# A two-layer network over spikes: the first layer on w1 rows gathered per batch, places by one-hot products

## The chip, the core and the metric

One Trainium2 chip, and of it one core. The program is launched once and the metric is its device time in microseconds (us). The core has five engines that run side by side: TensorE (PE) for matrix products, VectorE (DVE), ScalarE (ACT), GpSimd (POOL) and SyncE (SP), which here only issues DMAs. DMAs are issued from the queues of SP, ACT and POOL and run on 16 DMA engines.

## The reference

```python
def cond(inputs, initial_state):                 # inputs = x, (2, 2048, 512); initial_state (2, 512)
    rates = relu(inputs) * 0.001
    c = initial_state[:, None, :] + cumsum(rates, axis=1)
    fl = floor(c)
    prev = concatenate([floor(initial_state)[:, None, :], fl[:, :-1, :]], axis=1)
    return (fl - prev) / 0.001                    # a spike where a channel's sum crosses a whole number

def ffn(x, w1, b1, w2, b2):                       # w1 (512, 2048), w2 (2048, 512), all float32
    h = relu(einsum('bsd,dw->bsw', x, w1) + b1)
    return einsum('bsw,wd->bsd', h, w2) + b2

out = x + ffn(cond(x, cond_1024), w1, b1, w2, b2)
```

Each of the 1,024 channels (2 batches of 512) starts in [0, 1) and crosses a whole number at most about once in its 2,048 tokens. So most tokens have no spike and get one same row (the *idle row*, relu(b1) w2 + b2); a token with one spike gets the idle row plus a row of a table with one row per channel; only tokens where several channels cross together (*general* tokens, up to 128 *slots* in all) need the two layers.

## The kernel before

x lies in SBUF as `x_sb[b]`, 128 partitions of 16 tokens; a *block* is the 16 tokens of a partition. The steps:

- SP loads x and the pairs of w1 transposed and w2 (`w_pairs`), then b2, then w1 itself in four parts (L306).
- PE forms the table of 512 rows in PSUM (`ps_table`, `table_part`, L833): 16 chunks of 4 products of 128x128x512, two passes each. Between the parts it runs small products that find the crossings: block sums, the block of each channel, the token within it, counts per token (`count_tokens`), numbers of the general tokens (`count_before`), and the number given back to each channel (`give_back`).
- DVE finds for each channel the block (`find_blocks`), POOL gathers that block's 16 rates (L352), DVE finds the token (`find_tokens`) and the slot (`find_slots`; 0 for a channel that is alone). `first_spikes` and `second_spikes` (L634, L638) turn the slots of batch 0 and 1 into the one-hot matrix `spk_t`.
- After `second_spikes` DVE raises `adding` and adds the idle row to batch 0 and to half of batch 1 (`add_idle`, L697, from PSUM, 4 tokens a call); POOL, which waited for `adding`, does it for the other half of batch 1 (L364, a token a call). SP stores each quarter of a batch (L310, 1 MB, eight in all) in the written order (0,0) (0,1) (0,2) (0,3) (1,3) (1,0) (1,2) (1,1). A store waits for its quarter, and those behind it in SP's queue wait too.
- PE, after the table and w1: `first_layer` (L922, 16 chunks of four products of 128x128x128), in it `sum_rows` (rows of the slots), then `sum_checks`, then `second_layer` (L929, 16 products of 128x128x512). ACT applies relu between them (L466) and copies the four parts of the table out (L472).
- DVE between its calls of `add_idle`: `list_singles` (L646 to L653, where the table rows go), `find_members` (L658 to L661), `find_odd` and `count_crowd` (L665 to L672), `list_general` (L678 to L685, the rows of the slots), `judge`.
- POOL at the end, in this order: when batch 0 is stored, four scatter-adds of table rows into `out` (L357); the gather of the slots' rows of x (L376, `general_x`); when batch 1 is stored, four more scatter-adds; when the two layers are done, the scatter of the general rows (L387). SP waits for all of them.
- If a count shows that the shortcut does not hold, a slow path redoes every token (`redo`). It isn't taken with these inputs.

Each engine works its own list in order. `chain` makes an engine wait for the instruction just issued.

Of the kernel before, what the change touches and what calls it, by code (L numbers as in the profile page):

```python
# [18 lines left out]
def spike_ffn(nc, x, x_turned, cond, cond_cols, w1, w_pairs, b1_cols, b2, out):  # L19
# [35 lines left out]
    with ExitStack() as ctx:  # L55
# [27 lines left out]
        member = [sb(f"member{b}", [P, DC, P], BF16) for b in range(B)]  # L83
        facts = sb("facts", [P, NE, 3], BF16)
# [34 lines left out]
        batch_row = sb("batch_row", [P, NE])  # L119
        rates = sb("rates", [P, NE, BLK])  # L120
        climb = sb("climb", [P, NE, BLK])
        tokens_under = sb("tokens_under", [P, NE])
# [3 lines left out]
        slot = sb("slot", [P, NE])  # L126
# [9 lines left out]
        checks = sb("checks", [P, 2])  # L136
        slot_count = sb("slot_count", [P, 1])
        slot_place = sb("slot_place", [P, 2])
        slot_row = sb("slot_row", [P, 1])
        crowd = sb("crowd", [P, 1])  # L140
# [35 lines left out]
        ps_rows = ps_met[:, 4 * BLK + NE * 2 * BLK:4 * BLK + NE * 2 * BLK + 3]  # L176
# [7 lines left out]
        w1_in = [sem(f"w1_in{i}") for i in range(WQ)]  # L184
# [33 lines left out]
        members_ready = sem("members_ready")  # L218
# [12 lines left out]
        adding = sem("adding")  # L231
        idle_added = [[sem(f"idle_added{b}_{q}") for q in range(XQ)] for b in range(B)]
        idle_stored = [sem(f"idle_stored{b}") for b in range(B)]
        spk_ready = sem("spk_ready")
# [37 lines left out]
        def _(sp):  # L272
# [47 lines left out]
        def _(pool):  # L320
# [27 lines left out]
            for b in range(B):  # L348
                pool.wait_ge(sixteen_listed, b + 1)
                for c in range(DC):  # L350
# [3 lines left out]
                                            ).then_inc(sixteen_got[b], 16)  # L354

# [11 lines left out]

            pool.wait_ge(idle_copied, 1)
            pool.wait_ge(adding, 1)
# [21 lines left out]
            with pool.If(redo > 1):  # L391
                pool.wait_ge(singles_scattered, 16 * NE)
                pool.wait_ge(general_scattered, 16)
                pool.dma_start(own_init, cond.rearrange("(o b) d -> o b d", o=1).to_broadcast([P, B, D])).then_inc(
# [20 lines left out]
        def _(act):  # L415
# [614 lines left out]
```

## Time and profile before

| | us |
|---|---|
| median of 3 runs (lowest, highest) | 107.22 (106.98, 108.17) |
| the profiled execution | 108.13 |
| its span, first to last instruction | 106.4 |
| busy in the span: PE / DVE / POOL / ACT | 94.6 / 67.9 / 36.6 / 36.2 |

The profile is one execution. The span is what the engines' records cover; 1.73 us of the profiled execution lie outside it. Times of rows count from the start of the span. The busy time of an engine is a sum over stages, and a stage's end is read from what its last wait was for.

### The profile page before, as it was taken

Reading aid. Unit: us, or ns where it says so; the run is one execution under the profiler, and the core shown is the slowest. Engines: PE = TensorE matmul, PEld = TensorE weight load, DVE = VectorE, ACT = ScalarE, POOL = GpSimd, SP = SyncE. Lnnn points to the kernel's source line nnn. Section 1 sums busy time; section 2 is a strip of 40 time slices with the busy share of each in tenths; the row PEclk is TensorE's granted clock in tenths of the full one; section 3 lists DMA queues with packets and bytes.
Section 4 is the critical chain, followed back from the end, with each engine's and each line's share of the span. In section 5 each row is a group of like instructions: output and inputs, shape, how many; then the busy total and the mean of one; then the engine's idle time right before and its main releaser. Section 6 shows DMA issues by size and latency. Waiting matters only on the chain.

```text
span 106.4 us, 1159 instructions
## 1 busy us (share of the span) xinstructions
PE 94.6 (89%) x375; PEld 52.2 (49%) x375; DVE 67.9 (64%) x137; ACT 36.2 (34%) x66; POOL 36.6 (34%) x41
## 2 busy tenths in 40 slices
PE   5999999999999999999895999999999999995000
PEld 5844444444644444634251444599999644441000
DVE  2348999888599999385445599999998700022000
ACT  2867515514382353189740000059443200000000
POOL 6200000000077500038300199960018780088720
PEclk9999999999999999999999999999999999999965
DMA  2999999999999999999992000499999999947850
GB/s 90 276 351 407 421 419 411 405 410 411 407 408 408 395 391 413 398 390 386 374 367 91 0 0 6 197 441 397 434 404 397 391 202 354 242 93 99 103 108 9
DMA packets 10028, 31.66 MB, mean 298 GB/s; under 512 B 1671, under 2 KB 1799, under 8 KB 8994
## 3 DMA queue, kind: packets, MB, share of 16 engines
q1 hardware_dynamic: 8304, 29.63, 72.4%
q0 software_dynamic: 1568, 1.90, 10.9%
q8 instruction: 5, 0.08, 0.3%
q10 hardware_dynamic: 146, 0.01, 0.1%
q14 instruction: 5, 0.04, 0.1%
HBM read 21.58 MB, written 10.75 MB: 304 GB/s over the span
## 4 chain that ended last, share of the span: by engine, by line
PE 43%; DVE 15%; POOL 13%; issue 12%; DMA 10%; POOLq 2%; DVEq 0%
PE ps_table L833 37%; DVE x_sb L697 8%; POOL out L357 8%; DMA rates<-in_x_turned,sixteen_at 5%; DMA out<-x_sb 5%; DVE spk_t L638 4%; PE ps_small L934 4%; POOL rates L352 3%; PE ps_turn L870 2%; POOLq L55 2%; POOL out L387 1%; POOL general_x L376 1%; DVE under L579 1%; DVE blocks_under L582 1%; POOLq L267 0%
## 5 line engine op out<-in xcount | busy, mean ns | idle before, releaser
L833 PE MATMUL ps_table<-w_sb 128*128 128x512 f32 x128 | 57.5, 602 | 0.1
L833 PEld LDWEIGHTS ps_table<-w_sb 128*128 128x128 f32 x128 | 24.0, 193 | 27.0 <-issue 26.2
L352 POOL DMA_INDIRECT rates<-in_x_turned,sixteen_at x8 | 9.6, 1198 | 36.9 <-DVE sixteen_at L583 35.0
L428 ACT ACTIVATE w_sb<-w_sb,b_col 128x512 f32<-128x512 f32 (+2 forms) x19 | 12.2, 642 | 16.7 <-DMA w_sb<-in_w_pairs 16.7
L357 POOL DMA_INDIRECT out<-w_sb,to_single x8 | 12.5, 1561 | 15.7 <-DMA out<-x_sb 13.8
L569 DVE SCALAR_TENSOR_TENSOR total_two<-x_sb,total_two 128x1024 f32<-128x1024 f32 x14 | 17.1, 1224 | 1.1 <-DMA x_sb<-in_x 0.6
L929 PE MATMUL ps_table<-w_sb 128*128 128x512 f32 x32 | 14.0, 595 | 0.0
L697 DVE TENSOR_TENSOR x_sb<-x_sb,ps_idle 128x2048 f32<-128x2048 f32 x6 | 13.4, 2277 | 0.1
L364 POOL TENSOR_TENSOR x_sb<-x_sb,idle_row 128x512 f32<-128x512 f32 x8 | 10.1, 1289 | 9.1 <-DVEq L738 9.1
L429 ACT ACTIVATE w_sb<-w_sb,minus_relu_b 128x512 f32<-128x512 f32 (+2 forms) x19 | 12.3, 649 | 0.6
L929 PEld LDWEIGHTS ps_table<-w_sb 128*128 128x128 f32 x32 | 6.0, 190 | 7.2 <-issue 6.9
L466 ACT ACTIVATE w_sb<-ps_turn,b_col 128x128 f32<-128x128 f32 x8 | 2.9, 367 | 17.9 <-PE ps_turn L922 17.8
L922 PE MATMUL ps_turn<-spk_t,w_sb 128*128 128x128 f32 x64 | 8.5, 276 | 0.0
L922 PE MATMUL ps_small<-spk_t,w_sb 128*128 128x128 f32 x64 | 8.5, 275 | 0.0
L528 DVE SCALAR_TENSOR_TENSOR idle_part<-w_sb,relu_b,idle_part 128x512 f32<-128x512 f32 x9 | 6.8, 760 | 2.1 <-DMA w_sb<-in_w_pairs 2.0
L922 PEld LDWEIGHTS ps_turn<-spk_t,w_sb 128*128 128x128 f32 x64 | 7.9, 192 | 0.5 <-issue 0.5
L922 PEld LDWEIGHTS ps_small<-spk_t,w_sb 128*128 128x128 f32 x64 | 7.8, 192 | 0.0
L753 DVE TENSOR_TENSOR general_x<-general_x,b_row 128x512 f32<-128x512 f32 x1 | 0.7, 693 | 9.9 <-DMA general_x<-in_x,from_general 9.9
L934 PE MATMUL ps_small<-ones 128*128 128x128 f32 x16 | 3.8, 431 | 1.1 <-POOLq L329 1.1
L638 DVE SCALAR_TENSOR_TENSOR spk_t<-name_f,slot,spk_t 128x128 f32<-128x128 f32 x4 | 4.2, 1104 | 0.0
L466 ACT ACTIVATE w_sb<-ps_small,b_col 128x128 f32<-128x128 f32 x8 | 2.9, 367 | 3.2 <-PE ps_small L922 3.2
L934 PEld LDWEIGHTS ps_small<-ones 128*128 128x128 f32 x16 | 3.5, 330 | 1.1 <-POOLq L329 1.1
(124 smaller groups left out, 54.2 us busy)
## 6 DMA issues: line engine op xcount, KB each, us to landing
x_sb<-in_x SPq DMA_DIRECT2D x16, 512.0 KB, 14.3
out<-x_sb SPq DMA_DIRECT2D x8, 1024.0 KB, 4.8
w_sb<-in_w_pairs SPq DMA_DIRECT2D x15, 512.0 KB, 15.5
w_sb<-in_w SPq DMA_DIRECT2D x4, 1024.0 KB, 16.0
w_sb<-in_w_pairs SPq DMA_DIRECT2D x2, 256.0 KB, 3.1
b_row<-in_b SPq DMA_DIRECT2D x1, 256.0 KB, 15.6
rates<-in_x_turned,sixteen_at POOLq DMA_INDIRECT x8, 5.9
out<-w_sb,to_single POOLq DMA_INDIRECT x8, 6.6
```

The lines of the kernel that those rows point to most:

```text
L352: pool.indirect_dma_start(out=rates[:, col, :], out_offset=None, in_=x_sixteen, in_offset=bass.IndirectOffsetOnAxis(ap=sixteen_at[:, col:c ...
L357: pool.indirect_dma_start(out=out_rows, out_offset=bass.IndirectOffsetOnAxis(ap=to, axis=0), in_=row, in_offset=None, bounds_check=last_ro ...
L364: last = pool.tensor_tensor(x_sb[b][:, t, :], x_sb[b][:, t, :], idle_row[:, :], ALU.add)
L428: chain(act.activation(weights, weights, ACT.Relu, bias=b1_col[:, m:m + 1], scale=PER_DT))
L429: act.activation(weights, weights, ACT.Identity, bias=minus_relu_b1[:, m:m + 1]).then_inc(table_hidden_ready, 1)
L569: chain(dve.scalar_tensor_tensor(out=total_two[b][:, :, :], in0=tokens, scalar=0.0, in1=total_two[b][:, :, :], op0=ALU.max, op1=ALU.add))
L638: last = dve.scalar_tensor_tensor(out=spk_t[:, c, :], in0=slot_name, scalar=slot[:, DC + c:DC + c + 1], in1=spk_t[:, c, :], op0=ALU.is_equ ...
L697: last = dve.tensor_tensor(tokens, tokens, along(ps_idle[:, :], end - begin), ALU.add)
L833: last = pe.matmul(ps_table[c][:, :], table_hidden[:, m, c * P:(c + 1) * P], w2_sb[:, m, :], start=(m == 0), stop=(m == FC - 1))
L922: last = pe.matmul(ps_hidden[m % 2][:, 0:P], w1_sb[:, c, m * P:(m + 1) * P], spk_t[:, c, :], start=(c == 0), stop=(c == DC - 1))
L929: last = pe.matmul(ps_out[:, :], hidden[m], w2_sb[:, m, :], start=(m == 0), stop=(m == FC - 1))
L934: pe.matmul(ps_small[:, 0:P], ones[:, :], ones[:, :], start=True, stop=True)
```

## The change

w1 is no longer loaded whole (it is, from POOL, only on the slow path). For each batch, the channels that have a slot (*members*) get a *place* from 1 to 128: DVE counts them per partition (`count_members`), PE sums the counts over the partitions before, DVE makes a one-hot matrix of the places (`place_members`), PE multiplies it with the channel's facts (channel number, slot, row; `sum_places`), and DVE reads off for each place the row of w1, the token's row and a one-hot matrix of the slot (`list_places`). POOL gathers the 128 rows of w1 of each batch (8 KB each, 1 MB) by `get_w1`. The first layer is then two products a chunk, one for each batch (`general_first`), and runs two chunks ahead of the second (`general_second`), one after the other on PE.

Other things move. `spk_t` is not made outside the slow path. DVE starts `add_idle` after `list_places(1)`; `list_general` stands after the first call of `add_idle` and waits for `sum_rows`, which PE does between chunks 14 and 15 of the table; `list_singles` stands before the fourth call, `find_odd` and `count_crowd` after it. `adding` is gone: POOL issues `get_w1(0)`, `get_w1(1)` and the gather of `general_x` (which waits for `list_general`), and then adds its half of batch 1. ACT copies the first part of the table before the first relu, and `sum_checks` stands after chunk 5 of the second layer.

```diff
-            for i in range(WQ):
-                part = slice(i * (F // WQ), (i + 1) * (F // WQ))
-                sp.dma_start(w1_sb[:, :, part], w1.rearrange("(c p) f -> p c f", p=P)[:, :, part]).then_inc(w1_in[i], 16)
...
+            def get_w1(b):
+                pool.wait_ge(places_listed, b + 1)
+                pool.indirect_dma_start(out=w1_got_rows[b], out_offset=None, in_=w1,
+                                        in_offset=bass.IndirectOffsetOnAxis(ap=w1_at[b][:, :], axis=0)
+                                        ).then_inc(w1_got[b], 16)
...
+            get_sixteens(0)
+            get_sixteens(1)
+            get_w1(0)
             pool.wait_ge(idle_copied, 1)
-            pool.wait_ge(adding, 1)
+            get_w1(1)
+            pool.wait_ge(general_listed, 1)
+            pool.indirect_dma_start(out=general_x[:, :], out_offset=None, in_=x_rows,
+                                    in_offset=bass.IndirectOffsetOnAxis(ap=from_general[:, :], axis=0)
+                                    ).then_inc(general_got, 16)
             add_idle(1, 12, 16)
             add_idle(1, 8, 12)
             pool.wait_ge(singles_listed, 1)
             for b in range(B):
-                if b == 1:
-                    pool.wait_ge(general_listed, 1)
-                    pool.indirect_dma_start(out=general_x[:, :], out_offset=None, in_=x_rows,
-                                            in_offset=bass.IndirectOffsetOnAxis(ap=from_general[:, :], axis=0)
-                                            ).then_inc(general_got, 16)
                 pool.wait_ge(idle_stored[b], 16 * XQ)
...
+            act.wait_ge(table_summed, FC)
+            act.activation(table_row[0], ps_table[0][:, :], ACT.Copy).then_inc(table_rows_ready, 1)
             for m in range(FC):
-                if 1 <= m <= DC:
-                    act.activation(table_row[m - 1], ps_table[m - 1][:, :], ACT.Copy).then_inc(table_rows_ready, 1)
+                if 1 <= m < DC:
+                    act.activation(table_row[m], ps_table[m][:, :], ACT.Copy).then_inc(table_rows_ready, 1)
...
+                with nc.allow_low_precision(reason="whole numbers that the type holds"):
+                    chain(dve.tensor_reduce(facts_high[:, mine, 1:2].rearrange("p e o -> p (e o)"), slot_part[:, :, :],
+                                            AXIS.X, ALU.add))
+
+            def count_members(b):
+
+                mine = own(b)
+                chain(dve.tensor_scalar(is_member[:, mine], facts_high[:, mine, 1:2].rearrange("p e o -> p (e o)"), 0.5, None,
+                                        ALU.is_gt))
+                chain(dve.tensor_tensor_scan(member_run[b][:, :], ones[:, 0:DC], is_member[:, mine], 0.0, ALU.mult, ALU.add))
+                dve.sem_inc(members_counted, 1)
+                with nc.allow_low_precision(reason="whole numbers that the type holds"):
+                    chain(dve.tensor_reduce(facts_low[:, mine, 2:3].rearrange("p e o -> p (e o)"),
+                                            token_under[:, mine, 1:BLK], AXIS.X, ALU.add))
+
+            def place_members(b):
+                mine = own(b)
+                dve.wait_ge(members_before, b + 1)
+                chain(dve.scalar_tensor_tensor(out=place[:, mine], in0=member_run[b][:, :], scalar=ps_members[b],
+                                               in1=is_member[:, mine], op0=ALU.add, op1=ALU.mult))
+                chain(dve.tensor_tensor(place_hot[b][:, :, :], over(place[:, mine], P), along(slot_name, DC), ALU.is_equal))
+                dve.sem_inc(places_ready, 1)
+
+            def list_places(b):
+                dve.wait_ge(places_summed, b + 1)
+                dve.tensor_copy(w1_at[b][:, :], ps_places[b][:, 0:1]).then_inc(places_listed, 1)
+                dve.tensor_copy(place_fact[b][:, 1:2], ps_places[b][:, 2:3])
+                dve.tensor_scalar(place_slot[b][:, :], slot_name, ps_places[b][:, 1:2], None, ALU.is_equal).then_inc(
+                    slots_placed, 1)
...
-                chain(dve.tensor_reduce(tokens_under[:, :], token_under[:, :, 1:BLK], AXIS.X, ALU.add))
-                chain(dve.scalar_tensor_tensor(out=row_at[:, :], in0=blocks_under[:, :], scalar=float(BLK),
-                                               in1=tokens_under[:, :], op0=ALU.mult, op1=ALU.add))
+                chain(dve.tensor_tensor(row_at[:, :], facts_high[:, :, 2:3].rearrange("p e o -> p (e o)"),
+                                        facts_low[:, :, 2:3].rearrange("p e o -> p (e o)"), ALU.add))
                 chain(dve.tensor_scalar(not_single[:, :], met[:, :], 1.0, FAR, ALU.not_equal, ALU.mult))
-                chain(dve.tensor_tensor(row_at[:, :], row_at[:, :], batch_row[:, :], ALU.add))
                 dve.tensor_tensor(to_single[:, :], row_at[:, :], not_single[:, :], ALU.add).then_inc(singles_listed, 1)
-            def find_members():
-
-                for b in range(B):
-                    chain(dve.tensor_tensor(member[b][:, :, :], over(slot[:, own(b)], P), along(slot_name, DC), ALU.is_equal))
-                    chain(dve.tensor_scalar(facts[:, own(b), 1:2].rearrange("p e o -> p (e o)"), blocks_under[:, own(b)],
-                                            float(b * P), None, ALU.add))
-                chain(dve.tensor_copy(facts[:, :, 2:3].rearrange("p e o -> p (e o)"), tokens_under[:, :]))
-                dve.sem_inc(members_ready, 1)
...
+                chain(dve.tensor_scalar(under_zero[:, :], start_c[:, :], 0.0, float(2 * P), ALU.is_lt, ALU.mult))
+                chain(dve.scalar_tensor_tensor(out=over_two[:, :], in0=over_two[:, :], scalar=float(2 * P), in1=under_zero[:, :],
+                                               op0=ALU.mult, op1=ALU.add))
+                chain(dve.tensor_reduce(checks[:, 3:4], over_two[:, :], AXIS.X, ALU.add))
...
                 chain(dve.tensor_tensor(checks[:, 0:1], many_run[0][:, BLK - 1:BLK], many_run[1][:, BLK - 1:BLK], ALU.add))
+                for b in range(B):
+                    chain(dve.tensor_copy(checks[:, b + 1:b + 2], member_run[b][:, DC - 1:DC]))
                 dve.sem_inc(odd_ready, 1)
...
             find_slots(0)
-            first_spikes()
+            count_members(0)
+            place_members(0)
             find_tokens(1)
+            list_places(0)
             find_general(1)
             number_general(1)
             find_slots(1)
-            second_spikes()
-            dve.sem_inc(adding, 1)
+            count_members(1)
+            place_members(1)
+            list_places(1)
             add_idle(0, 0, 4)
+            list_general()
             add_idle(0, 4, 8)
             add_idle(0, 8, 12)
+            list_singles()
             add_idle(0, 12, 16)
-            list_singles()
-            find_members()
-            add_idle(1, 0, 4)
             find_odd()
             count_crowd()
-            list_general()
+            add_idle(1, 0, 4)
             add_idle(1, 4, 8)
             judge()
             dve.wait_ge(general_got, 16)
...
+            def count_members(b):
+                pe.wait_ge(members_counted, b + 1)
+                pe.wait_ge(sums_ready, B)
+                pe.matmul(ps_members[b], upper_b[:, :], member_run[b][:, DC - 1:DC], start=True, stop=True).then_inc(
+                    members_before, 1)
+            def sum_places(b):
+                pe.wait_ge(places_ready, b + 1)
+                for facts in (facts_high, facts_low):
+                    for c in range(DC):
+                        last = pe.matmul(ps_places[b], place_hot[b][:, c, :], facts[:, b * DC + c, :],
+                                         start=(facts is facts_high and c == 0), stop=(facts is facts_low and c == DC - 1))
+                last.then_inc(places_summed, 1)
+                pe.wait_ge(slots_placed, B)
+                for b in range(B):
+                    last = pe.matmul(ps_rows, place_slot[b][:, :], place_fact[b][:, :], start=(b == 0), stop=(b == B - 1))
                 last.then_inc(rows_summed, 1)
...
+            def general_first(m):
+                if m >= 2:
+                    pe.wait_ge(hidden_ready, m - 1)
+                for b in range(B):
+                    last = pe.matmul(ps_hidden[m % 2][:, 0:P], w1_got_rows[b][:, m * P:(m + 1) * P], place_slot[b][:, :],
+                                     start=(b == 0), stop=(b == B - 1))
+                last.then_inc(hidden_summed, 1)
+            def general_second(m):
+                if m == 0:
+                    pe.wait_ge(table_rows_ready, 1)
+                pe.wait_ge(hidden_ready, m + 1)
+                last = pe.matmul(ps_out[:, :], hidden[m], w2_sb[:, m, :], start=(m == 0), stop=(m == FC - 1))
+                if m == FC - 1:
+                    last.then_inc(out_summed, 1)
...
             give_back(0)
             turn_blocks(1)
-            table_part(12, 1, DC)
+            table_part(12, 1, 2)
+            count_members(0)
+            table_part(12, 2, 3)
+            sum_places(0)
+            table_part(12, 3, DC)
             count_tokens(1)
             table_part(13, 0, 1)
             count_before(1)
             table_part(13, 1, 2)
             give_back(1)
-            table_part(13, 2, DC)
+            table_part(13, 2, 3)
+            count_members(1)
+            table_part(13, 3, DC)
+            sum_places(1)
             table_chunk(14)
+            sum_rows()
             table_chunk(15)
+            pe.wait_ge(general_listed, 1)
+            for b in range(B):
+                pe.wait_ge(w1_got[b], 16)
+            general_first(0)
+            general_first(1)
+            for m in range(FC):
+                general_second(m)
+                if m + 2 < FC:
+                    general_first(m + 2)
+                if m == 5:
+                    sum_checks()
```

## Rows read from the trace of the kernel before

**Rows 1.** The page of the profile: the span.

```profile
span 106.4 us, 1159 instructions
```

**Rows 2.** Chain that ended last, in order of time: start us, us, what.

```profile
50.79 5.51 DMA rates<-in_x_turned,sixteen_at
...
73.64 4.97 DMA out<-x_sb
...
87.92 5.06 issue
...
100.67 1.03 POOL out L387
```

**Rows 3.** POOL in order of time: start us, us, instruction [idle before it <-releaser].

```profile
79.44 1.61 POOL L357 DMA_INDIRECT out<-w_sb,to_single  x1 [8.54 <-DMA out<-x_sb]
...
93.20 1.56 POOL L357 DMA_INDIRECT out<-w_sb,to_single  x1 [5.28 <-DMA out<-x_sb]
```

**Rows 4.** First and last store of `out` on SP, and their us to landing.

```profile
L310 SPq DMA_DIRECT2D out<-x_sb x1: 361/361/361, 67.0 to 67.0; - x1
...
DMA to landing us min/median/max: 4.0/4.0/4.0
...
L310 SPq DMA_DIRECT2D out<-x_sb x1: 332/332/332, 84.0 to 84.0; - x1
...
DMA to landing us min/median/max: 8.9/8.9/8.9
```

**Rows 5.** Stretches: us, busy of PE, PEld, DVE, ACT, POOL, PEclk, DMA share, GB/s.

```profile
57.00:67.00 10.00, 9.21 (x31) 4.19 (x32) 8.19 (x15) 0.00 (x0) 6.16 (x5) 1.00 0.01 4
...
69.00:93.00 24.00, 24.00 (x159) 18.73 (x159) 14.62 (x33) 7.82 (x20) 9.15 (x7) 1.00 1.02 361
...
71.00:79.00 8.00, 8.00 (x75) 8.00 (x74) 7.51 (x15) 5.21 (x13) 0.00 (x0) 1.00 1.02 424
```

**Rows 6.** DVE in order of time, columns as in rows 3.

```profile
13.67 0.75 DVE L528 SCALAR_TENSOR_TENSOR idle_part<-w_sb,relu_b,idle_part 128x512 f32<-128x512 f32 x1
...
64.75 8.87 DVE L697 TENSOR_TENSOR x_sb<-x_sb,ps_idle 128x2048 f32<-128x2048 f32 x4
...
73.54 0.28 DVE L646 TENSOR_TENSOR count_part<-ps_met,token_hot 128x128 f32<-128x128 f32 x1
...
75.09 0.17 DVE L653 TENSOR_TENSOR to_single<-row_at,not_single 128x8 int32<-128x8 f32 x1
...
75.18 0.68 DVE L658 TENSOR_TENSOR member<-slot,name_f 128x512 bf16<-128x512 f32 x1
...
79.57 0.16 DVE L665 TENSOR_TENSOR over_two<-block_sum,theta_sum 128x8 f32<-128x8 f32 x1
...
80.25 0.16 DVE L672 TENSOR_TENSOR checks<-many_run 128x1 f32<-128x1 bf16 x1
...
80.55 0.16 DVE L678 TENSOR_SCALAR slot_count<-ps_met 128x1 f32<-128x1 f32 x1
...
81.66 0.15 DVE L685 TENSOR_TENSOR to_general<-slot_row,none_far 128x1 int32<-128x1 f32 x1
```

**Rows 7.** Lines L638, L364, L697: ns min/median/max, first and last start us.

```profile
L638 DVE SCALAR_TENSOR_TENSOR spk_t<-name_f,slot,spk_t x4: 352/1352/1359, 60.6 to 63.5; 128x128 f32<-128x128 f32 x4
...
L364 POOL TENSOR_TENSOR x_sb<-x_sb,idle_row x8: 1265/1280/1318, 60.8 to 69.6; 128x512 f32<-128x512 f32 x8
...
L697 DVE TENSOR_TENSOR x_sb<-x_sb,ps_idle x6: 2273/2274/2287, 64.7 to 81.7; 128x2048 f32<-128x2048 f32 x6
```

**Rows 8.** PE in order of time, columns as in rows 3; two passes a float32 product.

```profile
59.94 8.83 PE L833 MATMUL ps_table<-w_sb 128*128 128x512 f32 x20
...
68.61 1.05 PE L922 MATMUL ps_turn<-spk_t,w_sb 128*128 128x128 f32 x8
...
79.33 0.34 PE L909 MATMUL ps_met<-facts,member 128*128 128x3 bf16 x8
...
83.33 13.98 PE L929 MATMUL ps_table<-w_sb 128*128 128x512 f32 x32
```

More of the change, by code:

```diff
@@ L82, in spike_ffn @@
         grid = [sb(f"grid{b}", [P, 2 * BLK], BF16) for b in range(B)]
-        member = [sb(f"member{b}", [P, DC, P], BF16) for b in range(B)]
-        facts = sb("facts", [P, NE, 3], BF16)
+        member_run = [sb(f"member_run{b}", [P, DC], BF16) for b in range(B)]
+        place_hot = [sb(f"place_hot{b}", [P, DC, P], BF16) for b in range(B)]
+        facts_high = sb("facts_high", [P, NE, 3], BF16)
+        facts_low = sb("facts_low", [P, NE, 3], BF16)
+        w1_at = [sb(f"w1_at{b}", [P, 1], I32) for b in range(B)]
+        place_fact = [sb(f"place_fact{b}", [P, 2]) for b in range(B)]
+        place_slot = [sb(f"place_slot{b}", [P, P]) for b in range(B)]
         spk_t = sb("spk_t", [P, DC, P])
@@ L175, in spike_ffn @@
         ps_back = ps_met[:, 4 * BLK:4 * BLK + NE * 2 * BLK].rearrange("p (e k) -> p e k", e=NE)
-        ps_rows = ps_met[:, 4 * BLK + NE * 2 * BLK:4 * BLK + NE * 2 * BLK + 3]
+        ps_rows = ps_turn[:, (B + 1) * BLK:(B + 1) * BLK + 2]
+        ps_members = [ps_turn[:, b:b + 1] for b in range(B)]
+        ps_places = [ps_turn[:, (b + 1) * BLK:(b + 1) * BLK + 3] for b in range(B)]
+        w1_got_rows = [w1_sb[:, b, :] for b in range(B)]
         ps_hidden = [ps_turn, ps_small]
@@ L183, in spike_ffn @@
         w2_first_in = sem("w2_first_in")
-        w1_in = [sem(f"w1_in{i}") for i in range(WQ)]
+        w1_in = sem("w1_in")
+        w1_got = [sem(f"w1_got{b}") for b in range(B)]
         start_in = sem("start_in")
@@ L596, in pick_blocks @@
                                   ALU.is_equal).then_inc(blocks_picked, 1)
+                chain(dve.tensor_scalar(facts_high[:, own(b), 2:3].rearrange("p e o -> p (e o)"), blocks_under[:, own(b)],
+                                        float(BLK), float(b * S), ALU.mult, ALU.add))
             def find_tokens(b):
@@ L630, in find_slots @@
                 chain(dve.tensor_tensor(slot_part[:, :, :], ps_back[:, mine, 0:BLK], token_hot[:, mine, :], ALU.mult))
-                chain(dve.tensor_reduce(slot[:, mine], slot_part[:, :, :], AXIS.X, ALU.add))
-            def first_spikes():
-                chain(dve.tensor_tensor(spk_t[:, :, :], over(slot[:, own(0)], P), along(slot_name, DC), ALU.is_equal))
-            def second_spikes():
-                for c in range(DC):
-                    last = dve.scalar_tensor_tensor(out=spk_t[:, c, :], in0=slot_name, scalar=slot[:, DC + c:DC + c + 1],
-                                                    in1=spk_t[:, c, :], op0=ALU.is_equal, op1=ALU.add)
-                    if c < DC - 1:
-                        last.then_inc(dve_step, 1)
-                steps[0] += DC - 1
-                last.then_inc(spk_ready, 1)
+                with nc.allow_low_precision(reason="whole numbers that the type holds"):
+                    chain(dve.tensor_reduce(facts_high[:, mine, 1:2].rearrange("p e o -> p (e o)"), slot_part[:, :, :],
+                                            AXIS.X, ALU.add))
@@ L963, in _ @@
             give_back(1)
-            table_part(13, 2, DC)
+            table_part(13, 2, 3)
+            count_members(1)
+            table_part(13, 3, DC)
+            sum_places(1)
             table_chunk(14)
+            sum_rows()
             table_chunk(15)
-            pe.wait_ge(spk_ready, 1)
-            for i in range(WQ):
-                pe.wait_ge(w1_in[i], 16)
-            for m, last in enumerate(first_layer(hidden_ready, 0)):
-                last.then_inc(hidden_summed, 1)
-                if m == 11:
-                    sum_rows()
-            sum_checks()
-            second_layer(hidden_ready, 0).then_inc(out_summed, 1)
+            pe.wait_ge(general_listed, 1)
[9 more added lines that the diff above has]
+                    sum_checks()
             pe.wait_ge(redo_ready, 1)
```

47 lines of the change are left out of this document (22 added, 25 removed).

## The prediction

> **What bounds the kernel now.** I read the span first [rows 1]: 106.4 us of the 108.13 of its execution, and then the chain of waits from its end. By busy time PE looks like the bound, but the end does not hang on PE. The last link is POOL's scatter of the general rows, issued at 100.67 [rows 2]; it stands behind four scatter-adds, which POOL begins at 93.20, when batch 1's stores have landed [rows 3]. The last store is issued at 84.03 and takes 8.9 us, so it lands at 92.9 [rows 4]. From that landing to the end of the span are 106.4 - 92.9 = 13.5 us, all POOL issue and the last landing. PE's second layer ends at 83.33 + 13.98 = 97.3 [rows 8], over 3 us before POOL could use it.
>
> Why does the last store take 8.9 us and the first 4.0 [rows 4]? The stretches tell: from 57 to 67 the DMA engines carry nothing (4 GB/s), from 69 to 93 they are full (share 1.02) [rows 5]. So the stores are a stream that a full DMA works off. Between 71 and 79, with stores alone, it moves 424 GB/s [rows 5]: 1.05 MB are 2.47 us a store, eight are 19.8. The first store's 4.0 us leave 1.5 beside its 2.47; I put 0.8 ahead of the data and 0.7 behind. Then data flow from 67.85 to 92.2, 24.4 us: 19.8 of stores and 4.6 of the batch 0 scatter-adds that go between them (POOL starts them at 79.44, when the store issued at 73.64 has landed [rows 2, 3]). Thus the end is: start of the stream, plus 24.4 if it never runs dry, plus 14.2. The question for each edit is whether the stream starts sooner, and whether it runs dry.
>
> **The change, part by part.**
>
> *w1's load goes, gathers come.* The 4.2 MB ended before 57 [rows 5], ten us ahead of the stores: nothing waited for them, gain 0. The rates' gather may land sooner than its 5.51 us [rows 2], but DVE is then busy with `place_members(0)` until about 56.1, against 56.4 before: 0 to 0.3, I take 0.2, spent in the next step.
>
> *From slots to stores.* Before, DVE had batch 1's slots at 60.6 and then four calls of L638 held it until 64.75 [rows 6, 7]. Now come two small DVE operations (0.2 each), a PE product (0.2), two DVE operations (0.25, and 0.68 for a 128x512 comparison [rows 6]), PE's eight small products (0.34 [rows 8]), `list_places` (0.45), with five hand-overs of 0.1: 2.6, to about 63.1. The first store is issued 2.25 later, at 65.35 instead of 67.05: 1.7 sooner.
>
> *PE meanwhile.* Table passes last 8.83 / 20 = 0.44 [rows 8]. Chunk 14 ended about 68.6 - 8 x 0.44 = 65.1; PE now waits some 0.3 at three or four of the added products, 0.9 together: 66.0. `sum_rows` 0.4: 66.4.
>
> *`list_general` moved up* stands behind the first `add_idle`, which ends at 65.35, and waits to 66.5, and then takes 80.55 to 81.8 = 1.26 [rows 6] less one operation, 1.05. Behind it waits the second `add_idle`: 67.55 to 69.8, and the third to 72.05 (2.2 a call [rows 6]). The stream, fed at 65.35, has its first store out by 68.6, or by 70.0 with the second w1 gather in its way (2.47 more), and gets the second from 70.65. Before, it had by then worked 2.8 us at stores, now 2.47: the lead of 1.7 is gone. The gather of `general_x` now also falls into the stream; by size a quarter of a store, 0.65.
>
> *POOL's half of batch 1 moves from 60.8 to 69.* It waits for `general_listed` (67.5), issues the gather (1.03 like L387 [rows 2]) and adds until 69 + 8 x 1.28 = 79.2. SP takes (1,3) and (1,2) only behind others, so that alone costs 0. What it meets costs: before, POOL added beside L638 and L697 only. The row of L638 shows what happens: the first call, ahead of POOL's, took 352 ns; the next three 1352 each, one POOL call (1280) apiece [rows 7], though the same operation on four times the columns takes 0.75 [rows 6]. L697 beside the same POOL calls was not slowed (2273 to 2287 in all six [rows 7]). L638 reads two tensors from SBUF, L697 one from SBUF and one from PSUM. So I expect that a DVE operation with two SBUF tensors waits for POOL's current call. In `list_singles` these are two (`row_at`, `to_single`), in `find_odd` and `count_crowd` three, two of them TENSOR_TENSOR and one of L638's own kind. Before, all of them ran with POOL silent, 0.17 each [rows 6].
>
> The Trainium skill, SBUF — State Buffer, section Who interferes with whom, says that a VectorE instruction with two SBUF inputs contends with a GpSimd one that reads SBUF, and the loser waits for the whole instruction; rows 7 agree for SCALAR_TENSOR_TENSOR. It extends this to `tensor_tensor` and, in a two-port mode, to `tensor_scalar`, which no row here shows; by it the sum below holds, and without it that of the first rival.
>
> Each wait lies between 0.2 and 1.28; the first of a group I take at half a call, 0.65, one behind another at 0.9. `list_singles` free: 73.54 to 75.26 is 1.72 [rows 6] for seven operations, five are left: 1.2, so 73.2; with the waits 74.8 (bounds 73.6 and 75.8). The fourth `add_idle` ends at 77.0 instead of 75.4. `find_odd` and `count_crowd`, 0.85 before [rows 6] and two copies more, 1.25, plus about 2 of waits until POOL ends at 79.5: 80.2. The last two calls end at 82.5 and 84.7 (before 79.6 and 84.0).
>
> *The stream again.* (0,1), (0,2) and `general_x` from 70.65: 76.2. (0,3), issued at 77.1, from 77.9: dry for 1.6. With (1,3) to 82.8. (1,0) from 83.2: dry 0.4. Then three stores, 7.4, and the scatter-adds' 4.6 (POOL begins them at 82.2, when (0,3) has landed): 95.2, landing 95.9. Before 92.9: +3.0, less the 0.2 of the rates: **+2.8**. The span would be 109.2. As the profiled execution lies 0.9 over the median of the runs shown, I set the change against the median: 107.22 + 2.8 = 110.0. With the waits' bounds +1.8 to +3.8.
>
> *The two layers.* A chunk is now four passes of 128 columns, 4 x 0.112 (L922's twelve chunks of eight passes lie between 68.61 and 79.33 [rows 8]), and two of 512 columns, 0.88: 1.32, times 16 is 21.2. It begins when the table ends, at 69.9, or the second w1 gather lands: 62.7 plus between 4.0 (a whole 1 MB store [rows 4]) and 5.5 + 2.5 (a small gather [rows 2] plus a store's data): 66.7 to 70.7; I take 70. `sum_checks` waits for `odd_ready` (80.2), PE stands about 1.5. End 93, against 97.3. That is 4 us gained where 3 were idle: worth 0. POOL issues the general scatter 100.67 - 92.9 = 7.8 us behind the last store's landing, so at 103.7: ten us of cover. If that were gone, each us of PE past it would be added.
>
> **Rivals.** *DVE does not wait for POOL* (L638's wait is its own kind's). Speaks for it that TENSOR_TENSOR with two SBUF tensors has no row beside POOL's adds. `add_idle` ends at 75.4, 78.95 and 81.2, the stream is dry only to 70.65, and its last data flow at 76.2 + 5 x 2.47 + 4.6 = 93.1, landing 93.8: +0.9, 108.1 (from +0.3 to +1.4, with one of L638's kind waiting).
>
> *The last store's landing follows its issue, not the backlog.* If the 8.9 us came from the scatter-adds' nearness alone, and DVE keeps clear of POOL, the last store is issued at 81.2 instead of 84.0 and the end comes 2.8 sooner: 104.4; faster from the point where the last `add_idle` ends before 82.9. Against it: the DMA share of 1.02 from 69 to 93.
>
> *The gather of w1 rows is far slower* (128 rows of 8 KB, some perhaps the same row), or DVE's waits are whole POOL calls each: past 111. The first decides only if the second gather lands after 80, ten us beyond the bounds.
>
> That the slow path is taken and w1 is loaded after all would show as hundreds of us; by the reference a channel rises 0.4 x 0.001 a token, so 512 cross 0.2 times a token and some 0.18 of about 420 crossings a batch meet another, near 76 members against 128 places: I leave it out.
>
> **Chances.** The forecast, DVE held by POOL and a stream run dry, 0.55 (109.0 to 111.0); DVE free 0.22 (107.5 to 108.6); landing follows issue 0.17 (104.4 to 106.1); worse 0.06. About 1% is what a measurement here can tell from no change, 106.15 to 108.3: slower gets the forecast, the worse cases and a third of the second, 0.68; same two thirds of the second, 0.15; faster the third, 0.17. The range holds the first two and the edges of the others: 106.6 to 111.3.
>
> **What the profile would show.** First store issued near 65.4, second near 69.8. POOL's adds from 69 to 79, and beside them DVE operations of 8 columns that last near 1 us instead of 0.17. DMA stretches that are not full near 69 to 70 and 77 to 78. Last store issued near 84.7, landing near 96, 13.5 before the end. PE's layers end near 93 with a wait for `odd_ready`. I am wrong if those small operations stay at 0.17, if the last store lands before 92, or if PE's end is the last wait.

## The result and the profile after

The changed kernel takes 111.34 us (median of 4 runs, 110.85 to 112.07), the kernel before 107.55 (4 runs): ratio 1.0356, 95% interval 1.0269 to 1.0444. It is slower, as forecast, but by 3.8 us and not by 2.8, and a little past the upper end of the range (111.3). The profiled execution took 110.85, its span is 109.1.

The end of the chain of waits (start us, us, what), which answers to [rows 2]:

```profile
66.82 4.39 DVE x_sb L724 x2
...
71.77 6.19 DVE row_at L686
...
78.37 6.92 issue
...
92.50 4.53 issue
...
104.66 1.03 POOL out L401
```

One VectorE operation, `row_at` in `list_singles`, stands in the chain with 6.19 us. Then "issue" 6.92: POOL waits until batch 0 is stored, and its last quarter, (0,3), is issued only at 80.6, behind the fourth `add_idle`, and takes 3.9 us to land. The tail is as before: POOL waits for the last store (the 4.53), scatters four times, and scatters the general rows.

VectorE in order of time (start us, us, instruction, in brackets idle time before it and what ended it), which answers to [rows 6]:

```profile
62.22 2.28 DVE L724 TENSOR_TENSOR x_sb<-x_sb,ps_idle 128x2048 f32<-128x2048 f32 x1
...
65.76 0.16 DVE L708 TENSOR_SCALAR slot_count<-ps_turn 128x1 f32<-128x1 f32 x1 [1.26 <-PE ps_turn L952]
...
66.73 4.48 DVE L724 TENSOR_TENSOR x_sb<-x_sb,ps_idle 128x2048 f32<-128x2048 f32 x2
71.13 0.29 DVE L684 TENSOR_TENSOR count_part<-ps_met,token_hot 128x128 f32<-128x128 f32 x1
...
71.77 6.18 DVE L686 TENSOR_TENSOR row_at<-facts_high,facts_low 128x8 f32<-128x8 bf16 x1
...
77.98 0.17 DVE L688 TENSOR_SCALAR not_single<-met 128x8 f32<-128x8 f32 x1
...
78.27 2.28 DVE L724 TENSOR_TENSOR x_sb<-x_sb,ps_idle 128x2048 f32<-128x2048 f32 x1
...
80.47 0.16 DVE L692 TENSOR_TENSOR over_two<-block_sum,theta_sum 128x8 f32<-128x8 f32 x1
```

`row_at` adds 8 columns of two SBUF tensors; the operations of this size in the kernel before took 0.17 [rows 6]. `count_part`, just ahead of it, has 128 columns, but one of its two inputs lies in PSUM, and it takes 0.29, as before (0.28). POOL in the same stretch, which answers to [rows 3] and to the row of L364 in [rows 7]:

```profile
68.06 9.85 POOL L376 TENSOR_TENSOR x_sb<-x_sb,idle_row 128x512 f32<-128x512 f32 x8
...
85.28 1.60 POOL L369 DMA_INDIRECT out<-w_sb,to_single  x1 [7.37 <-issue]
...
97.26 1.54 POOL L369 DMA_INDIRECT out<-w_sb,to_single  x1 [4.76 <-DMA out<-x_sb]
```

The eight adds run from 68.06 to 77.91, one about every 1.23 us, and `row_at`, which came at 71.77, as the third ended and the fourth began, ends at 77.95. It was held over all five that were left. The fourth `add_idle` of batch 0 stood behind it (78.27 instead of about 72.3), and with it the rest of the output. Stretches (us, busy of PE, PEld, DVE, ACT, POOL, granted clock, DMA share, GB/s), to set beside [rows 5]:

```profile
69.00:77.00 8.00, 7.66 (x36) 4.87 (x36) 7.93 (x5) 4.26 (x10) 8.00 (x8) 1.00 0.96 402
...
77.00:81.00 4.00, 1.80 (x11) 1.13 (x9) 3.86 (x8) 0.73 (x2) 0.92 (x1) 1.00 0.00 0
...
81.00:93.00 12.00, 11.21 (x45) 7.24 (x46) 6.07 (x10) 2.20 (x6) 6.30 (x4) 0.86 0.99 388
...
83.00:85.00 2.00, 2.00 (x7) 1.31 (x6) 2.00 (x2) 0.37 (x1) 0.00 (x0) 0.55 1.06 438
```

From 77 to 81 the DMA engines carry nothing, in the middle of the stream that was full from 69 to 93 before. The first store, (0,3) and the last one (SP; ns, start us, and us to landing), the first and last of which answer to [rows 4]:

```profile
L316 SPq DMA_DIRECT2D out<-x_sb x1: 348/348/348, 64.5 to 64.5; - x1
...
DMA to landing us min/median/max: 7.4/7.4/7.4
...
L316 SPq DMA_DIRECT2D out<-x_sb x1: 332/332/332, 80.6 to 80.6; - x1
...
DMA to landing us min/median/max: 3.9/3.9/3.9
...
L316 SPq DMA_DIRECT2D out<-x_sb x1: 623/623/623, 86.3 to 86.3; - x1
...
DMA to landing us min/median/max: 10.7/10.7/10.7
```

The last store lands at 86.3 + 10.7 = 97.0 and not at 92.9; the span ends 12.1 later.

### The profile page after: what moved, and what is told of

Its sections match the earlier page's. It is cut to its first block, busy times and chain, and to the rows that moved or that the text cites. A ratio compares the mean times of both kernels' runs of the same rounds, so it can differ in the third digit from the quotient of the medians.

```text
span 109.1 us, 1075 instructions
## 1 busy us (share of the span) xinstructions
PE 90.7 (83%) x325; PEld 46.1 (42%) x325; DVE 70.9 (65%) x148; ACT 36.5 (33%) x66; POOL 38.9 (36%) x43
## 4 chain that ended last, share of the span: by engine, by line
PE 46%; DVE 17%; issue 15%; POOL 10%; ACT 6%; POOLq 2%; DVEq 0%
PE ps_table L862 39%; POOL out L369 8%; DVE row_at L686 6%; DVE x_sb L724 4%; PE ps_small L993 3%; ACT w_sb L444 3%; ACT w_sb L443 2%; PE ps_turn L899 2%; POOLq L55 2%; DVE place_hot L673 1%; PE ps_idle L888 1%; POOL out L401 1%; DVE under L599 1%; ACT block_sum L453 1%; POOLq L277 1%
## 5 line engine op out<-in xcount | busy, mean ns | idle before, releaser
L862 PE MATMUL ps_table<-w_sb 128*128 128x512 f32 x128 | 58.0, 600 | 0.0
L862 PEld LDWEIGHTS ps_table<-w_sb 128*128 128x128 f32 x128 | 23.2, 190 | 24.2 <-issue 23.2
L443 ACT ACTIVATE w_sb<-w_sb,b_col 128x512 f32<-128x512 f32 (+2 forms) x19 | 12.2, 643 | 17.6 <-DMA w_sb<-in_w_pairs 17.5
L967 PE MATMUL ps_table<-w_sb 128*128 128x512 f32 x32 | 17.5, 634 | 0.1
L724 DVE TENSOR_TENSOR x_sb<-x_sb,ps_idle 128x2048 f32<-128x2048 f32 x6 | 13.5, 2282 | 0.1
L959 PEld LDWEIGHTS ps_small<-place_slot,w_sb 128*128 128x128 f32 x32 | 5.2, 209 | 3.9 <-issue 3.4
L959 PEld LDWEIGHTS ps_turn<-place_slot,w_sb 128*128 128x128 f32 x32 | 4.9, 197 | 4.4 <-issue 3.9
L784 DVE TENSOR_TENSOR w_sb<-ps_table,general_x 128x512 f32<-128x512 f32 x1 | 0.7, 692 | 8.8 <-PE ps_table L967 8.8
L686 DVE TENSOR_TENSOR row_at<-facts_high,facts_low 128x8 f32<-128x8 bf16 x1 | 6.2, 6178 | 0.0
L364 POOL DMA_INDIRECT w_sb<-in_w,w_at x2 | 1.9, 942 | 11.0 <-DVE w_at L678 11.0
L485 ACT ACTIVATE w_sb<-ps_table 128x512 f32<-128x512 f32 x1 | 0.6, 600 | 15.4 <-PE ps_table L862 15.4
L967 PEld LDWEIGHTS ps_table<-w_sb 128*128 128x128 f32 x32 | 5.4, 209 | 0.7 <-ACT w_sb L481 0.4
L959 PE MATMUL ps_turn<-place_slot,w_sb 128*128 128x128 f32 x32 | 5.2, 287 | 0.2 <-DMA w_sb<-in_w,w_at 0.2
L959 PE MATMUL ps_small<-place_slot,w_sb 128*128 128x128 f32 x32 | 5.3, 293 | 0.0
```

The lines of the kernel that those rows point to most:

```text
L443: chain(act.activation(weights, weights, ACT.Relu, bias=b1_col[:, m:m + 1], scale=PER_DT))
L686: chain(dve.tensor_tensor(row_at[:, :], facts_high[:, :, 2:3].rearrange("p e o -> p (e o)"), facts_low[:, :, 2:3].rearrange("p e o -> p (e ...
L724: last = dve.tensor_tensor(tokens, tokens, along(ps_idle[:, :], end - begin), ALU.add)
L862: last = pe.matmul(ps_table[c][:, :], table_hidden[:, m, c * P:(c + 1) * P], w2_sb[:, m, :], start=(m == 0), stop=(m == FC - 1))
L959: last = pe.matmul(ps_hidden[m % 2][:, 0:P], w1_got_rows[b][:, m * P:(m + 1) * P], place_slot[b][:, :], start=(b == 0), stop=(b == B - 1))
L967: last = pe.matmul(ps_out[:, :], hidden[m], w2_sb[:, m, :], start=(m == 0), stop=(m == FC - 1))
```

## The experiments

Two theories. **A**: the loss is the hold of one operation behind POOL's adds, which empties the stream of stores. **B**: the loss is what the change put into the stream and ahead of it, the two gathers of w1 rows, the early gather of `general_x` and the wait of `list_general`.

**e1_singles_first: `list_singles` into VectorE's idle time.**

```diff
             add_idle(0, 0, 4)
+            list_singles()
             list_general()
             add_idle(0, 4, 8)
             add_idle(0, 8, 12)
-            list_singles()
             add_idle(0, 12, 16)
```

> One call moved: the five operations of list_singles stand before list_general, where DVE stood idle for 1.26 us waiting for the rows of the slots, and POOL does not add there. Theory A (one VectorE operation, row_at, stood behind all of POOL's remaining adds for 6.18 us and emptied the stream of stores): row_at takes about 0.17; find_odd's first operation now meets POOL's adds at about 73.4 and stands until they end near 78, so that part of the loss stays: last store issued near 83.5 instead of 86.3, time 106.5 to 108.5 against 111.3 of the changed kernel. Rival B (the loss comes from what the change put in the DMA stream, two gathers of w1 rows and the early general_x gather, about 5.6 us of DMA work, and from the wait for list_general): none of that moves, 110.5 to 112.

107.53 us, ratio to the kernel before 1.0019 (0.9971 to 1.0067). One call of five small operations, moved, takes back the whole loss. The VectorE row that now meets POOL's adds:

```profile
74.19 4.64 DVE L692 TENSOR_TENSOR over_two<-block_sum,theta_sum 128x8 f32<-128x8 f32 x1
```

`over_two` has two float32 inputs from SBUF and is held as `row_at` was, 4.64 us, to the end of the adds. B is out as the main cause: all that it names is still there. The hold, too, is still there for another operation, but it comes only when the fourth `add_idle` is through, and (0,3) is issued at 74.3.

**e2_none_beside_pool: nothing with two SBUF tensors beside POOL's adds.**

```diff
             number_general(0)
+            find_odd()
             find_slots(0)
...
             place_members(1)
+            count_crowd()
             list_places(1)
             add_idle(0, 0, 4)
+            list_singles()
             list_general()
             add_idle(0, 4, 8)
             add_idle(0, 8, 12)
-            list_singles()
             add_idle(0, 12, 16)
-            find_odd()
-            count_crowd()
             add_idle(1, 0, 4)
```

> As the run before, and find_odd stands behind number_general(0) and count_crowd behind place_members(1), where DVE waited for PE, so that no DVE operation with two SBUF inputs stands beside POOL's adds. Theory A: the five calls of add_idle follow one another from 66.8 to 77.8, the stream is not dry after 64.5, PE's wait of 3 us for odd_ready is gone (worth nothing for the end); 106.0 to 107.8. Theory B: 110.5 to 112.

105.86 us, ratio 0.9863 (0.9814 to 0.9913): below both kernels. VectorE's five adds in one piece, the stretches, and the first and last rows of PE's layers:

```profile
67.65 11.07 DVE L724 TENSOR_TENSOR x_sb<-x_sb,ps_idle 128x2048 f32<-128x2048 f32 x5
...
69.00:77.00 8.00, 7.28 (x34) 4.35 (x32) 8.00 (x5) 3.90 (x9) 8.00 (x7) 1.00 1.00 415
...
77.00:81.00 4.00, 4.00 (x21) 2.57 (x20) 2.50 (x5) 1.10 (x3) 1.87 (x2) 1.00 1.02 428
...
81.00:93.00 12.00, 11.38 (x51) 6.72 (x49) 0.83 (x2) 2.94 (x8) 6.38 (x5) 1.00 1.03 367
...
70.70 0.68 PE L959 MATMUL ps_turn<-place_slot,w_sb 128*128 128x128 f32 x4 [0.61 <-DMA w_sb<-in_w,w_at]
...
90.50 1.88 PE L967 MATMUL ps_table<-w_sb 128*128 128x512 f32 x4
```

Five calls of `add_idle` take 11.07, though POOL adds beside them from 68.98 to 78.87: with one tensor from SBUF and one from PSUM nothing is held. The stream is full from 69 to 93. PE's two layers take 70.7 to 92.4, 21.7 us against 28.7 before; yet of the 7 us nothing is seen at the end, which still comes its tail behind the last store.

**e10_one_gather: what is left of B.** The kernel of e2 without the second gather:

```diff
-            get_w1(1)
...
-w1_got_rows[b][:, m * P:(m + 1) * P]
+w1_got_rows[0][:, m * P:(m + 1) * P]
...
-            for b in range(B):
-                pe.wait_ge(w1_got[b], 16)
+            pe.wait_ge(w1_got[0], 16)
```

> The kernel of e2_none_beside_pool without the second gather of w1 rows: PE takes the first batch's rows for both (so the general rows of batch 1 are not the reference's). What is left of rival B: the gather's 1 MB stands in the DMA stream between 65 and 68 and delays all stores. If the stream is never dry, its 2.5 us come off the end: 103.0 to 104.2 against 105.9 of e2_none_beside_pool. If the stream has slack of its own later on, 104.5 to 106.

104.46 us, ratio 0.9734 (0.9680 to 0.9788), against 0.9863 for e2: about 1.4 us (0.6 to 2.2 by the two intervals), not 2.5. So B holds for a part: the gather stands in the stream, but without it the stream has a gap of its own, since the first store has landed by 69.6 and the second is issued at 70.0. Its first store, with no gather ahead of it, lands as fast as in [rows 4]:

```profile
L316 SPq DMA_DIRECT2D out<-x_sb x1: 348/348/348, 65.7 to 65.7; - x1
...
DMA to landing us min/median/max: 3.9/3.9/3.9
```

**Why five adds and not one?** I had put a wait at no more than one POOL call, as the row of L638 showed it in the kernel before. Four runs looked for the difference.

*e4_other_op: the kind of operation.*

```diff
-chain(dve.tensor_tensor(row_at[:, :], facts_high..., facts_low..., ALU.add))
+chain(dve.scalar_tensor_tensor(out=row_at[:, :], in0=facts_high..., scalar=1.0, in1=facts_low...,
+                               op0=ALU.mult, op1=ALU.add))
```

and the same for `to_single`, `over_two` and the first of `count_crowd`.

> The four TENSOR_TENSOR operations with two SBUF inputs that stand beside or just behind POOL's adds (row_at, to_single, over_two, the first of count_crowd) become SCALAR_TENSOR_TENSOR of the same inputs (times 1.0 first); the order stays. In the kernel before, three SCALAR_TENSOR_TENSOR got in between POOL's adds, one an add (1.35 us each). If the kind of operation decides whether it gets in, row_at takes at most 1.4 here, to_single also, and the time is 107 to 109. If not, row_at takes about 6 again and the time is about 111.3.

111.0 us. The kind makes no difference:

```profile
71.92 6.18 DVE L686 SCALAR_TENSOR_TENSOR row_at<-facts_high,facts_low 128x8 f32<-128x8 bf16 x1
```

*e3_pool_earlier: POOL's adds from 64 to 73.*

```diff
+            add_idle(1, 12, 16)
+            add_idle(1, 8, 12)
             pool.wait_ge(general_listed, 1)
             pool.indirect_dma_start(out=general_x[:, :], ...)
-            add_idle(1, 12, 16)
-            add_idle(1, 8, 12)
```

> In the changed kernel POOL's eight adds stand ahead of the wait for general_listed and the gather of general_x, so they run from 64 to 74 and not from 68 to 78. Theory A in the form that the first runs gave it (any VectorE operation with two SBUF inputs that comes while POOL adds stands until POOL's adds are over): row_at is hardly held any more, as it comes at about the end of them, but the last operation of list_general, to_general, which has two SBUF inputs, comes at 66.7 and is held to 74; the second add_idle stands behind it, the stream is dry from about 69 to 76, PE's general_first and the gather of general_x wait for general_listed too: 111.5 to 114. If row_at alone is prone (its two-byte inputs): to_general takes 0.15, and the time is 106.5 to 108.

112.2 us (two runs), ratio 1.0452 (1.0354 to 1.0551). Now `row_at` comes when POOL's adds are over and takes 0.17, and the operation that is held is the last of `list_general`, one column wide:

```profile
66.49 6.94 DVE L713 TENSOR_TENSOR to_general<-slot_row,none_far 128x1 int32<-128x1 f32 x1
...
78.39 0.17 DVE L686 TENSOR_TENSOR row_at<-facts_high,facts_low 128x8 f32<-128x8 bf16 x1
```

Operations of 1 and 8 columns, with two-byte and four-byte inputs, have now been held alike (e5 adds one of 128 columns). Common to them is that they have two SBUF tensors and come while POOL adds.

*e5_probe: L638's own operations in that place, and eight POOL adds more.*

```diff
+            for t in range(8):
+                pool.tensor_tensor(w1_sb[:, 2 + t // 4, ...], b2_row[:, :], idle_row[:, :], ALU.add)
...
+            probe()        # L638's four, then one of them, then a tensor_tensor of 128 columns
             list_singles()
```

> The changed kernel with a probe of the hold itself: POOL does eight adds more (into a part of w1's tile that is unused, from the rows of b2 and the idle row), so it adds for some 20 us from 68 on; and DVE, ahead of list_singles, does the four operations of L638 in their own form (128 columns, a pointer scalar, no wait between them), then one of them alone behind a wait, then a TENSOR_TENSOR of 128 columns behind a wait, and then list_singles as it was, whose row_at has 8 columns. If length or a pointer scalar lets an operation in between two adds, the first five take 1.3 each and only row_at is held; if being queued without a wait does it, only the second to fourth take 1.3 and the next one is held; if what mattered before was that L638 began ahead of POOL's first add, the first operation here is held to the end of the adds, near 88. The time is 113 to 125 in all cases and says nothing.

VectorE's row of the four (ns min/median/max, first and last start us), and POOL's sixteen adds:

```profile
L689 DVE SCALAR_TENSOR_TENSOR spk_t<-name_f,place,spk_t x4: 337/338/16702, 71.4 to 88.5; 128x128 f32<-128x128 f32 x4
...
68.32 9.87 POOL L376 TENSOR_TENSOR x_sb<-x_sb,idle_row 128x512 f32<-128x512 f32 x8
...
78.15 9.78 POOL L393 TENSOR_TENSOR w_sb<-b_row,idle_row 128x512 f32<-128x512 f32 x8
```

The run takes 123.31 us. The first of the four is held 16.70 us, from 71.4 in POOL's third add to the end of the adds near 88; the next three take 0.34. The same operations that got in between the adds in the kernel before are held here over the rest of one and thirteen more. There the first of them had begun ahead of POOL's first add.

*e6_pool_one_by_one: a wait between POOL's adds.*

```diff
                     last = pool.tensor_tensor(x_sb[b][:, t, :], x_sb[b][:, t, :], idle_row[:, :], ALU.add)
                     if t % TQ == TQ - 1:
                         last.then_inc(idle_added[b][t // TQ], 1)
+                        pool.wait_ge(idle_added[b][t // TQ], 1)
+                    else:
+                        chain(last)
```

> The changed kernel with POOL's adds apart: each waits for the one ahead of it. In the probe POOL's adds began 1.23 us apart and lasted 1.28, so one began before the other had ended, and the first VectorE operation with two SBUF inputs was held 16.7 us over all of them; in the kernel before, beside L638, they began 1.27 apart. If it is this overlap that leaves no gap, row_at now gets in after at most one add (1.4 us or less), to_single and the operations of find_odd too, and the time is 106.5 to 109. If an operation that comes after POOL has begun is held until POOL has nothing more to do, row_at takes about 6 again and the time is 111 to 112.5.

108.55 us, ratio 1.0162 (1.0099 to 1.0224), against 1.0356 for the change as it is. VectorE's five operations with two SBUF tensors, and POOL's adds:

```profile
72.34 0.29 DVE L689 TENSOR_TENSOR row_at<-facts_high,facts_low 128x8 f32<-128x8 bf16 x1
...
72.87 1.12 DVE L692 TENSOR_TENSOR to_single<-row_at,not_single 128x8 int32<-128x8 f32 x1
...
76.11 0.59 DVE L695 TENSOR_TENSOR over_two<-block_sum,theta_sum 128x8 f32<-128x8 f32 x1
...
76.82 1.23 DVE L698 SCALAR_TENSOR_TENSOR over_two<-over_two,under_zero 128x8 f32<-128x8 f32 x1
...
78.28 1.11 DVE L703 TENSOR_TENSOR checks<-many_run 128x1 f32<-128x1 bf16 x1
...
68.63 10.74 POOL L376 TENSOR_TENSOR x_sb<-x_sb,idle_row 128x512 f32<-128x512 f32 x8
```

Each gets in after at most one add: 0.29, 1.12, 0.59, 1.23, 1.11, where the same order of VectorE's program without the wait had one hold of 6.18. The adds together take 10.74 instead of 9.85, 0.9 more for the waits and the operations let in. So what held `row_at` was that POOL's adds follow one another without a gap: in the kernel as it is one add begins about 1.23 after the other and lasts 1.26. It is not the whole rule, since L638 in the kernel before got in between adds as close; what differed there is that its first operation had begun ahead of them, and no run takes that apart.

**e8_before_apart: the same contention in the kernel before.** L638 ran beside POOL's adds because `adding` was raised when its four operations had been issued, not when they were done: POOL's first add began at 60.84, while the first of the four still ran (60.65 to 61.00).

```diff
                 last.then_inc(spk_ready, 1)
+                dve.wait_ge(spk_ready, 1)
```

> The kernel before with one wait more: DVE raises adding, which starts POOL's adds, only when the four operations of L638 are done, and not while they run. Theory A: they take about 0.3 each instead of 1.35, the first store is issued 3 us sooner (64 instead of 67), the stream ends 3 us sooner, and the end then stands behind PE's second layer (97.3, its row at 98.1), so 2 to 2.8 us are gained: 104.7 to 105.6 against 107.5. Rival: 1.1 to 1.35 is what those operations take for themselves: no change, or the extra wait added.

104.93 us, ratio 0.9788 (0.9723 to 0.9853): the fastest but for e10, which leaves a gather out. Its rows of VectorE and of POOL's last scatter:

```profile
60.01 1.14 DVE L638 SCALAR_TENSOR_TENSOR spk_t<-name_f,slot,spk_t 128x128 f32<-128x128 f32 x4
...
96.78 0.69 DVE L756 TENSOR_TENSOR w_sb<-ps_table,general_x 128x512 f32<-128x512 f32 x1 [5.00 <-PE ps_table L930]
...
97.80 1.03 POOL L387 DMA_INDIRECT out<-w_sb,to_general  x1 [0.30 <-DVE w_sb L756]
```

L638's four operations take 1.14 together instead of 4.18, and 2.5 us of the 3 arrive at the end. The last scatter comes 0.30 behind the one ahead of it, as all of POOL's scatters do; but VectorE's sum of PE's second layer, which it needs too, is done only at 97.47, when POOL's scatter ahead of it ends. So here PE's end is the next limit: a further gain at the stores would stop at it, unless the first layer got shorter too, and no run tries that.

**e0_before: the kernel before, a second profile.**

> The kernel before once more, for a second profile on the chip of the runs beside it: 107.4; by theory A the three of L638 that stand beside POOL's adds take 1.35 each again.

108.18 us, span 106.4; L638's row:

```profile
60.99 4.17 DVE L638 SCALAR_TENSOR_TENSOR spk_t<-name_f,slot,spk_t 128x128 f32<-128x128 f32 x4
```

The four take 4.17 again, against 4.18.

## Why the prediction was right or wrong

**Right: what bounds.** The end stays a tail behind the last store's landing: 13.5 us before, 12.1 after, 12.2 in e2 and 12.6 in e8, though their last stores land between 90.1 and 97.0. The store stream is what counts, and a stream run dry is what the change costs (DMA share 0.00 from 77 to 81; none in e2).

**Right: the parts that were to be worth nothing.** w1's load: nothing waited for it, and its going is not seen. The rates landed sooner, worth 0.2 at most, as the slots' rows lie 1.0 sooner than in the trace of before, of which 0.84 were there already when POOL began the gather (45.83 against 46.67). That start varies by itself: it is 47.04 in e0 and 45.95 in e8, whose programs are alike up to there. PE's gain, too: off the path by 8 us.

**Right in size: from slots to stores.** The first `add_idle` began 2.6 behind the slots (59.61 to 62.22; forecast 2.6; the terms listed add up to 2.8, and the 0.2 of the rates that make the difference are taken off a second time at the end of the sum), VectorE waited 1.26 for `sum_rows` (forecast 1.15), the w1 gather landed at 69.4 (bounds 66.7 to 70.7, 70 taken).

**Wrong: the price of the hold.** The step that failed is "each wait lies between 0.2 and 1.28". It took L638's row, one add for one operation, for the rule. The first operation was held over all of POOL's adds that were left, 6.0 us, and the four others not at all, since by then POOL had done. Forecast were 1.6 ahead of (0,3) and 2 behind it; it was 6 and 0. So (0,3) was issued at 80.6 instead of 77.1, the stream was dry for nearly 5 us instead of 2.0, and the last store landed at 97.0 instead of 95.9, in a trace that had begun 0.84 sooner. e6 shows the term itself: with gaps between the adds the waits come to 0.12 + 0.95 + 0.43 + 1.06 + 0.94 = 3.5, where I had 3.6. The Trainium skill, SBUF — State Buffer, section Who interferes with whom, says that a VectorE instruction with two SBUF inputs contends with a GpSimd one that reads SBUF; the traces agree, with TENSOR_TENSOR (6.18 us) as well as SCALAR_TENSOR_TENSOR (16.70 us in e5), and not for one with a PSUM input (2.2 to 2.3 us a call of `add_idle`, beside POOL's adds or not). The Trainium skill, the same page, section Summary: rules for kernel authors, says that the second one to issue is blocked until the first has finished. Here it was blocked over a whole sequence of the other engine's instructions, and the measurement decides.

**Wrong, and hidden by it: the level.** The forecast span, 109.2, is the measured one, 109.1, by errors that cancel. The tail was 12.1 and not 13.5: the scatter of the general rows ends the span 4.4 behind its issue instead of 5.7. In e2 it is 4.6, in e8 4.9, and why it differs isn't settled. And the trace of before was of an execution late by 0.84 in its first 46 us; taken from there, the change costs 2.7 + 0.84 = 3.5, near what the medians say (3.8). e6 puts a size on both errors: there the five waits take what was forecast, and the loss is 1.7 us (1.1 to 2.4 by its interval) and not 2.8. So other terms were some 1.1 too high, and the hold beyond its price cost the other 2.1. e6's tail is 12.2 (94.4 to 106.6), which can be most of the 1.1; the rest isn't taken apart. That the time came so near the range is in part luck.

**The rivals.** That VectorE does not wait for POOL, or only in L638's kind of operation, is refuted by `row_at` itself, by `over_two` in e1 and by `to_general` in e3. The worse case, which had each wait at a whole POOL call and a chance of 0.06, named the right term, but what came was one wait of five calls and four of none. That the landing follows the issue and not the backlog: in e2 the last store was issued at 79.3, 4.8 us sooner than before, and landed 13.3 later, at 92.6 against 92.9: refuted. PE and the gathers came in time. The stores of e2 (first and last start us, and us to landing; the longest is the last store's):

```profile
L316 SPq DMA_DIRECT2D out<-x_sb x8: 332/338/1126, 65.7 to 79.3; - x8
...
DMA to landing us min/median/max: 6.2/8.1/13.3
```

**PE's clock**, not forecast: PE stood 2.99 us for `odd_ready` (forecast 1.5), and the stretch from 83 to 85 shows a granted clock of 0.55, most of it at the lower level (1.2 GHz), against 1.00 ahead of it. PE's layers ended at 96.1 instead of 93; the scatter that needs them was issued at 104.66, so it cost nothing.

```profile
81.79 0.39 PE L974 MATMUL ps_table<-checks,ones 128*128 128x4 f32 x2 [2.99 <-DVEq L703]
...
94.23 1.88 PE L967 MATMUL ps_table<-w_sb 128*128 128x512 f32 x4
```

## What to carry to other kernels

Look for VectorE operations with two SBUF tensors that fall beside a run of GpSimd operations on SBUF: one of 8 columns can stand for all that is left of the run, and all behind it in VectorE's queue with it. Either place them where GpSimd is silent (in idle time that is there anyway, as in e1 and e2), let one operand come from PSUM, or put a wait between GpSimd's instructions (e6). Where a semaphore starts GpSimd, let it rise when VectorE's operations are done and not when they are issued (e8). And before speeding up an engine, follow the chain back from the end: here PE got 7 us shorter and the end, hanging on stores that VectorE feeds, did not see it.

## What the runs showed of the hardware that I had not expected

- An operation held by GpSimd isn't let in when the current GpSimd instruction ends, if the next follows without a gap: 6.18 us over five adds, 16.70 over thirteen and part of one. With a wait between the adds it is 1.23 at most. Where VectorE's first operation had begun ahead of GpSimd's first add, the following ones got in one by one at 1.35 each. What makes that case different from a gap isn't shown: there too the adds' records lie close (10.05 for eight, against 9.85).
- A gather of 128 rows of 8 KB lands in 6.5 us with nothing else on the DMA engines, and in the stream of stores it costs about 1.4 us of the end, less than a store of the same size takes (2.5).
